# Layer 0 of a four-layer network: the order of work on VectorE and TensorE inside a turn is rewritten

## The reference, cut to what matters

```python
xn = _layernorm(x)
x1 = _mqa(xn) + xn                      # 16 heads of 8, one shared key and value head, causal softmax
xr = x1 @ w_in; u0, res = halves of xr  # 2 x 256 channels
u = silu(conv(u0, 4 taps) + conv_b)
x_dbl = u @ w_xproj                     # 8 for delta, 16 for B, 16 for C
delta = softplus(x_dbl[:8] @ w_dt + b_dt)
h = exp(delta*A)*h + (delta*u)*B        # over the tokens, 256 channels x 16 states
y = (sum over states of h*C + u*Dp) * silu(res)
x = x + x1 + y @ w_out                  # the mixture of experts of layer 0 is added later
```

## Time and profile before

| | |
|---|---|
| runs | 3720.51 us median, 3714.95 to 3730.46 |
| profiled execution | 3708.94 us, span 3707.3 us |
| layer 0 within it | about 45 to 1301.7 us |
| one turn of layer 0 in steady state | 75.1 us |
| busy in that turn | TensorE 54.9, VectorE 58.9, ScalarE 29.1, GpSimd 21.4 us |
| granted TensorE clock in that turn | 0.82 of full speed |

### The profile page before, as it was taken

One profiled execution on the slowest core, in us unless ns is written; L12 is line 12 of the kernel. 1 busy time (PEld: TensorE's weight loads), 2 busy tenths in 40 slices (PEclk: granted clock), 3 DMA queues, 4 the chain that ended last, 5 costly groups with the idle time before them and its releaser, 6 DMA issues.

```text
span 3707.3 us, 46620 instructions
## 1 busy us (share of the span) xinstructions
PE 2903.1 (78%) x17705; PEld 2057.2 (55%) x17705; DVE 2334.3 (63%) x4713; ACT 1411.3 (38%) x3560; POOL 818.0 (22%) x453
## 2 busy tenths in 40 slices
PE   4777777777766595999999999976888886667666
PEld 2455545554544394666666666654565555445444
DVE  3588788777876713665656666554544442888887
ACT  1443343334433200554545454531333332444443
POOL 0032223222232500222222222220000000333332
PEclk9887888788888755898989999985777777888887
DMA  1001000100010051000000000000000001343342
GB/s 50 19 28 37 29 24 24 37 33 24 24 35 35 29 180 73 1 1 1 1 1 1 1 1 1 1 28 11 21 18 17 6 16 50 132 133 123 133 135 84
DMA packets 71343, 147.90 MB, mean 40 GB/s; under 512 B 6864, under 2 KB 37072, under 8 KB 70608
## 3 DMA queue, kind: packets, MB, share of 16 engines
q1 hardware_dynamic: 69072, 140.73, 11.3%
q0 software_dynamic: 2048, 4.20, 0.4%
HBM read 135.20 MB, written 9.18 MB: 39 GB/s over the span
## 4 chain that ended last, share of the span: by engine, by line
PE 49%; DVE 25%; issue 14%; POOL 7%; ACT 3%; DMA 1%; SPq 0%; POOLq 0%; DVEq 0%; ACTq 0%
DVE h L1464 7%; PE psum L503 5%; PE psum L543 5%; POOL h L2032 4%; PE psum L281 4%; DVE mx L1349 3%; PE psum L611 3%; PE psum L615 3%; DVE h L1456 3%; PE psum L523 2%; PE psum L771 2%; POOL h L1998 2%; PE psum L731 2%; PE psum L622 2%; PE psum L379 2%
## 5 line engine op out<-in xcount | busy, mean ns | idle before, releaser
L1998 POOL TENSOR_TENSOR h<-h,Crep 128x1024 f32<-128x1024 f32 x128 | 352.7, 2761 | 941.0 <-DVE h L1464 941.0
L1980 POOL TENSOR_TENSOR pr<-pr,rsum 128x512 f32<-128x512 f32 x192 | 242.0, 1260 | 815.5 <-DVE rsum L1306 815.5
L1464 DVE TENSOR_TENSOR_SCAN h<-dA,h 128x1024 f32<-128x1024 f32 x128 | 363.6, 2845 | 0.7
L1802 ACT ACTIVATE pt<-psum 128x1024 f32<-128x1024 f32 x192 | 190.2, 1019 | 396.7 <-PE psum L622 389.2
L771 PE MATMUL psum<-h,pack_wf 128*128 128x256 f32 x1024 | 294.0, 442 | 56.7 <-POOL h L1998 56.7
L1349 DVE TENSOR_REDUCE mx<-psum 128x4 f32<-128x1024 f32 (+1 forms) x192 | 225.0, 1212 | 100.8 <-PE psum L620 100.8
L771 PEld LDWEIGHTS psum<-h,pack_wf 128*128 128x128 f32 x1024 | 224.0, 228 | 111.9 <-POOL h L1998 68.2
L1759 ACT ACTIVATE pr<-psum,nb 128x256 f32<-128x256 f32 (+1 forms) x512 | 208.4, 417 | 170.3 <-DVE nb L1298 169.5
L503 PE MATMUL psum<-kT,qT 64*128 64x256 f32 (+1 forms) x1024 | 249.1, 381 | 3.3 <-ACT pr L1759 3.3
L2032 POOL TENSOR_TENSOR h<-h,Crep 128x1024 f32<-128x1024 f32 x64 | 150.5, 2351 | 385.6 <-DVE h L1215 385.6
L1456 DVE TENSOR_TENSOR h<-dtu,psum 128x512 f32<-128x512 f32 x256 | 163.6, 679 | 105.6 <-PE psum L783 105.6
(11 more groups left out here) (334 smaller groups left out, 5794.7 us busy)
## 6 DMA issues: line engine op xcount, KB each, us to landing
Crep<-c_rows SPq DMA_DIRECT2D x64, 512.0 KB, 3.7
Brep<-bc_rows SPq DMA_DIRECT2D x64, 512.0 KB, 6.1
Crep<-bc_rows SPq DMA_DIRECT2D x64, 512.0 KB, 6.0
w1r<-m_w SPq DMA_DIRECT2D x32, 256.0 KB
w2r<-m_w SPq DMA_DIRECT2D x32, 256.0 KB
pack_wf<-wf SPq DMA_DIRECT2D x1, 3192.0 KB, 10.6
slots<-zero SPq DMA_DIRECT2D x12, 256.0 KB, 3.0
w1s<-s_w SPq DMA_DIRECT2D x8, 256.0 KB
```

The lines of the kernel that those rows point to most:

```text
L1464: ve.e.tensor_tensor_scan(flat(h), flat(k.dA[c][r]), flat(h), 0.0, ALU.mult, ALU.add).then_inc(*k.set("scanned", 0, b, g, c))
L1980: po.e.tensor_tensor(p3, p3, bcast(k.rsum[u % 3][:, 0:len(heads)], P * (q + 1), 2), ALU.mult).then_inc(*k.set("normed", l, b, u))
L1998: po.e.tensor_tensor(h[:, :, :], h[:, :, :], k.Crep[n % 3][:, :, :], ALU.mult).then_inc(*k.set("hC", 0, b, g, c))
```

## The change

Only layer 0's order and staging change; every instruction that computes something stays, with the same shapes. `out` moves one turn later (sequence t-1 in turn t), the reading of the sums and y_out move to a new stage `results` (t-3), the products of group 0 and one spread of group 1 move to the end of the turn before, and the last sums move to the beginning of the next turn. Turns 0 to 18 exist. The results of w_in go to bank 4 (that of `out`) and those of y_out to bank 5, where it was 5 and 7. All yields get new numbers, the two scans of a group stand nearer together, products and maxima stand behind them, and the fixed pattern of `GROUP_AT` becomes tables:

```diff
-TURN = {0: 60, 2: 24, 3: 37}
+TURN = {0: 57, 2: 24, 3: 37}
...
+OUT_AT = {0: (0.3, 5, 8.3, 8.9, 10, 11.7, 13.7, 14.3), 2: (0, 3, 6, 7, 8, 9)}
+MAX_AT, KEYS_AT = (1, 13.75, 30), (10.9, 23.5, 41.5)
+PV_AT = {0: (31, 47), 2: (10.5, 17)}
+MAX_TURN_AT = {0: 50, 2: 19}
...
-GROUP_AT = (2, 15, 28, 41)
+SCANS_AT = ((0, 2.3), (14.5, 17.4), (28, 31.7), (42.7, 46.4))
+SPREADS_AT = ((0.5, None, -1), (6.6, 1, 1), (9.7, 2, 0), (13.8, None, 0), (18.2, 2, 1), (23.4, 3, 0), (24.4, None, 1), (30.5, 3, 1),
+              (38.7, None, 2), (40.3, 4, 0), (50, 4, 1), (52.4, 5, 0))
+PRODUCTS_AT = ((5.2, 1, 0), (8.3, 1, 1), (19.6, 2, 0), (22.1, 2, 1), (34, 3, 0), (37, 3, 1), (48.7, 4, 0), (51, 4, 1))
+MAXIMA_AT = ((0, 0, 6.5), (0, 1, 9.6), (1, 0, 20.9), (1, 1, 23.4), (2, 0, 38.3), (2, 1, 40.2))
+DECAYS_AT = ((0.8, 2.6, 1), (21, 23, 2), (34, 36, 3), (46.5, 48.3, 4))
...
 def pe_inner(k, b):
-    yield 1
-    bk = pe_take(k, 0)
+    yield 14.6
     pe.wait_ge(*k.at("x1T", b))
...
-    yield 4
-    bk = pe_take(k, 0)
+    yield 17.6
+    pe.wait_ge(*k.at("zc", b, 0))
...
-    yield 18
+    yield 29.5
     u = k.su[b % 2]
...
-    yield 26
+    yield 37.3
...
+def pe_results(k, b):
+    yield 13.1
+    bk = pe_take(k, 0)
     pe.wait_ge(*k.at("yT", b))
...
 def sp_layer0(k):
     for t in range(NB + 2):
-        for g in (1, 2):
-            if 0 <= t - 2 < NB:
-                sp_c_spread(k, t - 2, g)
-        if 0 <= t - 1 < NB:
-            sp_c_store(k, t - 1)
-        if t + 1 < NB:
-            sp_negmax(k, 0, t + 1)
         if 0 <= t - 2 < NB:
             sp_c_spread(k, t - 2, 3)
         if 0 <= t - 1 < NB:
+            sp_c_store(k, t - 1)
             sp_c_spread(k, t - 1, 0)
+            sp_c_spread(k, t - 1, 1)
+        if t + 1 < NB:
+            sp_negmax(k, 0, t + 1)
+        if 0 <= t - 1 < NB:
+            sp_c_spread(k, t - 1, 2)
```

More of the change, by code:

```diff
@@ L322, in pe_pre0 @@
     k.pre_read = ("qk_ve", 0, b, 1)
-    yield 34
+    yield 46
+    bk = pe_take(k, 0)
+    pe.wait_ge(*k.at("gv", b))
+    for q in range(QT):
+        i = pe.e.transpose(bk[:, q * E0:(q + 1) * E0], k.PT[:, b, q * P:(q + 1) * P], w["ident"][0:E0, 0:E0])
+    i.then_inc(*k.set("gv_turned", b))
+    k.pre_read = ("gvT", b)
+    yield 48
+    bk = pe_take(k, 0)
+    for q in range(QT):
+        i = pe.e.matmul(bk[:, 0:E0], xn[:, q, :], k.gvT[:, q, :], start=q == 0, stop=q == QT - 1)
+    i.then_inc(*k.set("merged_mm", b))
+    k.pre_read = ("merged", b)
+    yield 51.1
     bk = pe_take(k, 0)
@@ L714, in pe_wide, with pe_wide0 @@
         pe_max_turn(k, l, b + 1)
+def pe_wide0(k, l, b):
+    for c in range(3):
+        yield MAX_AT[c]
+        if b + 1 < NB:
+            pe_quad(k, 0, "max", b + 1, c)
+        yield KEYS_AT[c]
+        pe_quad(k, 0, "keys", b, c)
+        if c:
+            yield PV_AT[0][c - 1]
+            pe_pv(k, 0, b, c - 1)
+    yield MAX_TURN_AT[0]
+    if b + 1 < NB:
+        pe_max_turn(k, 0, b + 1)
 def pe_first_max(k, l):
@@ L755, in pe_inner, with pe_spread, pe_sums @@
     k.pre_read = ("zin", 0, b)
-GROUP_AT = (2, 15, 28, 41)
-def pe_states(k, b):
-    pe, w, SB, YB = k.pe, k.w, k.bank[SPREAD_BANK], k.bank[Y_BANK]
-    def add_up(g, c):
+SCANS_AT = ((0, 2.3), (14.5, 17.4), (28, 31.7), (42.7, 46.4))
[4 more added lines that the diff above has]
+DECAYS_AT = ((0.8, 2.6, 1), (21, 23, 2), (34, 36, 3), (46.5, 48.3, 4))
+def pe_spread(k, b, g, j):
+    pe, w, SB = k.pe, k.w, k.bank[SPREAD_BANK]
+    pe.wait_ge(*k.at("split", 0, b))
+    was = (b, g, 0) if j else (b, g - 1, 1) if g else (b - 1, 3, 1) if b else None
+    if was is not None:
+        pe.wait_ge(*k.at("dbu", 0, *was))
+    for m in range(2):
+        i = pe.e.matmul(SB[:, m * L:(m + 1) * L], w["sel"][:, g * NG + 2 * j + m, :], k.split[b % 2][:, :], start=True, stop=True)
+    i.then_inc(*k.set("spread", 0, b, g, "B", j))
+def pe_sums(k, b, g):
+    pe, w, YB = k.pe, k.w, k.bank[Y_BANK]
+    for c in range(CI):
         h = k.h[c][g % 2]
@@ L773, in add_up, with pe_states @@
         i.then_inc(*k.set("summed", 0, b, g, c))
[L775 to L792, removed]
+def pe_states(k, b):
+    for at, g, j in SPREADS_AT:
+        yield at
+        if g is None and 0 <= b + j // 4 < NB:
+            pe_sums(k, b + j // 4, j % 4)
+        if g is not None and 0 <= b + g // 4 < NB:
+            pe_spread(k, b + g // 4, g % 4, j)
+def pe_results(k, b):
+    pe, w = k.pe, k.w
+    yield 13.1
+    bk = pe_take(k, 0)
     pe.wait_ge(*k.at("yT", b))
@@ new lines, in ve_product @@
+def ve_product(k, b, g, j):
+    ve, SB = k.ve, k.bank[SPREAD_BANK]
+    was = (b, g - 2) if g >= 2 else (b - 1, g + 2) if b else None
+    ve.wait_ge(*k.at("dtu", b))
+    ve.wait_ge(*k.at("spread", 0, b, g, "B", j))
+    for c in range(CI):
+        if was is not None:
+            ve.wait_ge(*k.at("summed", 0, *was, c))
+        i = ve.e.tensor_tensor(k.h[c][g % 2][:, 2 * j:2 * j + 2, :], bcast(k.dtu[b % 2][:, c, :], 2, 1),
+                               SB[:, :].rearrange("p (n t) -> p n t", n=2), ALU.mult)
+    i.then_inc(*k.set("dbu", 0, b, g, j))
@@ new lines, in ve_scan @@
+def ve_scan(k, b, g, c):
+    ve, h = k.ve, k.h[c][g % 2]
+    ve.wait_ge(*k.at("dA", 0, b, g, c))
+    ve.wait_ge(*k.at("dbu", 0, b, g, 1))
+    ve.e.tensor_tensor_scan(flat(h), flat(k.dA[c][g % 2]), flat(h), 0.0, ALU.mult, ALU.add).then_inc(*k.set("scanned", 0, b, g, c))
+def ve_states(k, b):
+    steps = [(SCANS_AT[g][c], g, c, True) for g in range(4) for c in range(CI)]
+    steps += [(at, g, j, False) for at, g, j in PRODUCTS_AT]
+    for at, g, n, scan in sorted(steps):
+        yield at
+        if scan and 0 <= b < NB:
+            ve_scan(k, b, g, n)
+        if not scan and 0 <= b + g // 4 < NB:
+            ve_product(k, b + g // 4, g % 4, n)
@@ L1466, in ve_states, with ve_results @@
+def ve_results(k, b):
+    ve, w, YB, su = k.ve, k.w, k.bank[Y_BANK], k.su[b % 2]
+    yield 10.8
     ve.wait_ge(*k.at("summed", 0, b, 3, 1))
@@ L1832, in ac_wide, with ac_wide0 @@
         ac_max_taken(k, l, b + 1)
+def ac_wide0(k, l, b):
+    for c, at in enumerate((12.6, 26.8, 44.3)):
+        for h in range(2):
+            yield at + h
+            ac_exp(k, 0, b, c, h)
+        if c:
+            yield (32.5, 50)[c - 1]
+            ac_heads_taken(k, 0, b, c - 1)
+    yield 51
+    if b + 1 < NB:
+        ac_max_taken(k, 0, b + 1)
 def ac_out(k, l, b, at):
```

178 lines of the change are left out of this document (72 added, 106 removed).

## The result

The changed kernel takes 3551.8 us (median of 4 runs, 3540.6 to 3554.5) against 3717.7 us: ratio 0.9544, 95% interval 0.9511 to 0.9577. The forecast was 3590, with 3500 to 3680 as its range. The profiled execution takes 3554.5 us with a span of 3552.9, 154 us less than before.

The account below looks back on a forecast made before the run. A ring of waits between VectorE's and TensorE's in-order lists was taken as the bound. Turns from 75.05 to 66 us gave 109, with the edges 125, off 3708.9: 3584, taken as 3590 us; range 3500 to 3680.

Parts of the forecast that it names:

- new lists with old durations: Whole turn: follow the changed instruction lists using durations measured before; 64.8 us, taken as 66 us a turn.
- the chain: The turn followed item by item through VectorE's and TensorE's new lists, from group 0's first scan to 64.8 us.
- 0 to 14.3: Turn's start: VectorE sets the time, scans through L1473; GpSimd works from 4.5 to 9.2 beside steps reading PSUM.
- 14.3 to 27.5: From L1473 to spread (2,1): TensorE's list sets the time, 13.2 us; VectorE idles 3.1 us.
- my signs: Predicted trace marks: turn 64 to 68 us, VectorE busy about 56, one 4.4 us scan in groups 1 and 2.
- u between the scans of group 2: u has two SBUF inputs and parts the scans, so GpSimd gets in again, until 42.4 us.
- rival A: VectorE keeps the ports when a small step parts scans: 2.2 at u, 1.4 at dtu; 62.4 a turn; chance 0.15.
- Spread (3,1): TensorE waits there for product (3,0) from about 39.5; pv and block 2 queue behind, so VectorE idles 2.2 us.
- my prices for half rate: TensorE's lower clock costs 1.3 us on half the sums, 1.4 on w_in, 1.0 to 1.9 on a block.
- rival C: TensorE's clock stays lower: 75.2 to 77.2 us a turn, chance 0.07; half of it, 68 to 74, chance 0.17.
- The edges: Turns outside the twelve: turns 14 to 17 gain 9, 7, 3 and 1 us; turns 0 and 1 cost 4.
- The half of the 11.6 us: Whole time: the median lay 11.6 us above the profiled execution; half was added on top of 3584, giving 3590.

Follow-up runs that it names:

- the pair alone in the old order: The kernel before with only each group's second scan placed directly behind the first in VectorE's list: 3748.8 us, ratio 1.0062.
- the run with xn first: The changed kernel with xn ahead of the first scan of group 1 instead of between the two: 3560.1 us, ratio 0.9562.
- the early spread: The changed kernel with spread (2,1) moved right behind w_in's first part, ahead of xn turned and w_in's second part: 3565.3 us, ratio 0.9576.
- sums first: The changed kernel with the sums of group 0 ahead of block 1 of the maxima in TensorE's list: 3509.7 us, ratio 0.9426.

## Why the prediction was right

*The method, new lists with old durations,* came out at 64.8 us a turn before I added for the clock; measured 64.85. That they meet this closely is luck, as parts of it were off and cancelled; that the turn lies in the forecast's 64 to 68 us is not luck alone, as every step came within 3 us of the chain. From the turn's first scan:

| step | predicted | measured |
|---|---|---|
| L1473 done | 14.3 | 13.9 |
| product (2,1) can start | 27.5 | 30.4 |
| scan (2,0) starts | 34.7 | 37.5 |
| scan (2,1) done | 42.4 | 43.0 |
| maxima of block 2 start | 48.6 | 48.5 |
| end | 64.8, taken as 66 | 64.85 |

*0 to 14.3:* right, and the reading behind it (steps that read PSUM go beside GpSimd) is shown by the pair's rows, by the pair alone in the old order, and by the cut of GpSimd's work.

*14.3 to 27.5:* TensorE's list set the time, as said, through the items named. It came 2.9 us later, because y_out, block 1 and the sums ran at 1.2 GHz (2.08, 3.05 and 5.39 instead of 1.16, 1.8 and 3.8). I had put the slow stretch behind spread (3,1); it is here, and there are three. GpSimd got in at xn as said, but it was xn's second instruction that was held (2.61), not the scan behind it, and without effect on the turn, as the run with xn first shows. So of my signs, one scan of 4.4 us in groups 1 and 2 did not come, and VectorE is busy 53.0 us where I had about 56.

*u between the scans of group 2:* I said that GpSimd would get in, as at X. It did not: 7.73 us for its two, and the scan had its 2.27. This is rival A for one of its places, -2.2 us. In every steady turn VectorE goes first behind PT (before) and u (after), and GpSimd behind X and sig (before) and xn (after). The 32 partitions of PT are not the reason, as u has 128. What is remains open. The rule of the Trainium skill quoted in the prediction (page "SBUF — State Buffer", section "SBUF: two separate sides"), that whoever starts first has the ports, does not tell the order in the rows of u either: GpSimd asks at 658.24, ahead of the scan at 659.20, and the scan still goes first.

*Spread (3,1):* I had TensorE stand there for 4 us. It does not wait at all: at 662.93 it comes right behind bc, since TensorE was late by its slow stretch. Block 2 therefore cost VectorE 1.1 instead of 2.2 us of idle time. Part of my 2.2 was a misreading: I took pv as 2.4 us at either clock, but the row lies in a slow stretch (granted 0.53 from 554.6 to 557.1). The same kernel has it at full clock, and the changed kernel's pv in this place takes 1.51 as well:

```profile
568.87 1.51 PE L659 MATMUL psum<-pt,v 128*32 128x256 f32 x32
```

w_in's 5.04 us and the 3.17 of the sums in the earlier trace rows lie only partly in slow stretches, so my prices for half rate were too low: a whole half of the sums at half rate took 3.78 in the run with 18 extra matmuls.

*Clock:* rival C at a part of its size. The granted clock fell from 0.82 to 0.79 although TensorE's busy share rose from 73% to 88%. I had allowed 1.2 us a turn for it.

*The edges* were sized too small at both ends: turns 14 to 18 gave 35 us where I had 20, probably since TensorE has less to do there (63, 51, 52 and 43 us from first scan to first scan, for 65, 58, 55 and 47), and the start cost 12 where I had 4. With 128 instead of 109 in between, that is 151 instead of 125 in layer 0. The half of the 11.6 us that I added for the median did not come either: the median lies 3 us under the profiled execution.

## What to carry to other kernels

Behind an instruction that releases GpSimd, put VectorE's steps that read PSUM, not ones with all inputs in SBUF; putting another such step there only shifts the hold to it. Follow the changed lists with measured durations, item by item, before believing a table of planned times: that gave the turn to 2% here, some of it by errors that cancelled. When an edit gains nothing, look first at the next wait behind it: the gate's exponential took what the early spread gave. Then look at TensorE's clock and try neighbouring orders, as a swap of two adjacent items was worth 1.2%. And read in the trace how long extra work really is before concluding from it.

## What was not expected of the hardware

The steady turn takes preferred lengths: 75.09 us before, 64.85 in three kernels with different lists, 61.44 in two (sums first; GpSimd's work cut). In those kernels the slow stretches of TensorE's clock begin at the same place in each turn, as all else does. Where they do not, the turns differ by 1 to 4 us from one to the next, often in a pattern: two turns with extra matmuls ahead of y_out (63.8 and 65.9), five with the sums first and the early spread (60.5, 61.2, 61.3, 63.6 and 63.95). That the clock causes this is not shown. That the slow stretches cost time is supported by the run with extra matmuls in five places (0.93, 2 us less with 11.4 us more work); the two other runs with extra matmuls put work on the path and decide nothing. Extra work that fits the idle time was not run.
